# A graph network kernel: sheaves of 2048 sorted edges passed by one-hot products, in place of most row gathers

## The chip, the cores and the metric

The kernel runs on one core of a Trainium2 chip. The metric is device time in microseconds from start to end of one execution, median over runs; lower is better.

## The reference, cut to what matters

Four graph networks run one after the other on 6250 nodes of 128 features and 100,000 edges that are sorted by destination; each ends in a residual and a layer norm. Only the edge passing matters here:

```python
def _L0_gnn_ref(...):            # two passes of 64 features
    agg = jax.ops.segment_sum(h[src] * norm[:, None], dst, num_segments=n)
def _L1_gnn_ref(...):            # one pass of 128 features
    aggregated = jax.ops.segment_sum(x[src], dst, num_segments=num_nodes)
def _L2_gnn_ref(...):            # five layers of 128 features, with edge attributes
    for l in range(num_layer):
        m = jax.nn.relu(h[src] + edge_attr)
        agg = jax.ops.segment_sum(m, dst, num_segments=n)
def _L3_gnn_ref(...):            # two attention layers; the change leaves them alone
    ...
```

`src` is random, `dst` rises.

## The kernel before

Edges lie in 782 tiles of 128, nodes in 49 blocks of 128. A **pair** is an edge tile with a node block that it touches; there are at most 830, padded to 832, in 208 **groups** of four. A **stage** (one call of `_mixed`) is one edge passing: it reads a table of node rows in memory and adds into an aggregate in the SBUF. There are eight: two of 64 features ("narrow", L2225 and L2228), one of 128 (L2235) and five of 128 with attributes ("edge", L2261). Two attention stages (`_converse`, `_attend`) follow.

In a stage each group goes through the engines in this order. ACT copies four index columns (`index`, L1433). POOL issues four indirect DMAs, one per pair, each of which fetches 128 rows of the table (`fetch`, L1414). In edge stages SP loads four tiles of attributes (`load_attr`, L1387), DVE adds them (`join`, L1548) and ACT applies relu (L1450). ACT makes for each pair the matrix that tells which edge belongs to which node (`select`, L1441 to L1444). PE multiplies (`scatter`, L1509: four f32 matmuls, two instructions each) and DVE adds each pair's result to its node block (`add`, L1598). Rings of four buffers join the steps; semaphores named `index`, `gathered`, `joined`, `message`, `select`, `product` and `added` order them.

Some groups, 28 of 208 in a narrow stage and 18 in a wide one, fetch no rows by DMA. The table lies in the SBUF too, split into three bf16 terms (`first`, `second`, `high`, `middle`), and PE picks the rows with one-hot products: for each of the 49 blocks DVE makes a one-hot (L1580) and PE runs four matmuls of 384 (192) columns (`expand`, L1522); DVE sums the three terms (`merge`). These products are spread between the other groups' work. The groups of a stage's lead (10 or 12) run ahead of the loop while the table is split.

`_walk` finds the pairs and `_degree` counts degrees before the first stage; `_table` and `_norm` write a table to memory between stages. Each engine's work is a program of its own, in order, written out in the sequence in which it runs; `_hold` waits on a semaphore, with the target computed in a register inside loops. `_words` loads numbers from the SBUF into registers; such a number in an address (`bass.ds(where, 1)`) is computed in the sequencer.

## Time and profile before

| | us |
|---|---|
| median of 3 runs | 11302.24 (11300.65 to 11303.89) |
| the profiled execution, span | 11311.4 |
| PE busy | 8547.4 (76%) |
| DVE busy | 7592.0 (67%) |
| POOL busy | 7703.4 (68%) |
| ACT busy | 6350.9 (56%) |

The profiled execution is one run with the profiler on; its span is from the first to the last instruction and there is nothing of note around it, so it stands 9 us above the median. Busy time counts an engine's instructions. "PEld" is the loading of weights, which overlaps matmuls. "issue" after idle time means that the profile shows nothing that the engine waited for. Engine names with a q (PEldq, DVEq) are the sequencers, whose register work isn't counted as busy.

### The profile page before, as it was taken

The numbers are of one execution on the slowest core, as the hardware profiler recorded it, in microseconds if no ns is written. First come the engines' busy times: TensorE is split into PE (matmuls) and PEld (weight loads), VectorE is DVE, ScalarE is ACT, GpSimd is POOL, SyncE is SP. The second block draws the span as 40 slices with busy tenths as digits, with TensorE's granted clock in tenths as the row PEclk, the third lists the DMA queues.
The fourth block names the chain that finished last, engine by engine and source line by source line (L and its number), as shares of the span: only waits on it lengthen the run. The fifth ranks groups of instructions, "written<-read, shape, count | busy, mean of one in ns | idle before, by whom it ended". The sixth has DMA issues, their size and how long they took to land. (4 is left out here: it accounts for less than half of the span.)

```text
span 11311.4 us, 289275 instructions
## 1 busy us (share of the span) xinstructions
PE 8547.4 (76%) x56139; PEld 6348.4 (56%) x56140; DVE 7592.0 (67%) x21896; ACT 6350.9 (56%) x16860; POOL 7703.4 (68%) x7879
## 2 busy tenths in 40 slices
PE   5888688688868886887788688868886566656665
PEld 2777577555546554655555455645564455545554
DVE  5787678655557666776677666767775566746667
ACT  4444454444455555555555555555555666646774
POOL 2777777677757766775777577757773777657774
PEclk7999799799979997999899899989997787868887
DMA  2111111222234434443444344434443666546663
GB/s 57 31 31 30 38 32 31 53 56 56 55 92 111 110 92 113 112 111 89 116 110 111 96 110 111 112 95 112 111 108 101 180 193 193 149 132 189 197 194 113
DMA packets 1311535, 1169.02 MB, mean 103 GB/s; under 512 B 239258, under 2 KB 1106238, under 8 KB 1310224
## 3 DMA queue, kind: packets, MB, share of 16 engines
q0 software_dynamic: 272544, 566.00, 19.9%
q1 hardware_dynamic: 1038256, 596.28, 18.1%
q14 instruction: 647, 5.30, 0.1%
q8 instruction: 88, 1.44, 0.1%
HBM read 1009.04 MB, written 152.40 MB: 103 GB/s over the span
## 5 line engine op out<-in xcount | busy, mean ns | idle before, releaser
L1414 POOL DMA_INDIRECT rings<-rows_key,idx x4536 | 4361.0, 961 | 1919.5 <-issue 1333.9
L1598 DVE TENSOR_TENSOR bigDE<-bigDE,part 128x128 f32 (+1 forms) x6656 | 1891.0, 284 | 1398.1 <-PE part L1509 419.3
L1509 PE MATMUL part<-rings 128*128 128x128 f32 (+1 forms) x11920 | 1712.5, 290 | 658.8 <-ACT rings L1450 257.7
L1522 PE MATMUL wide<-bigDE,bigC 128*128 128x384 bf16 x10800 | 1951.6, 338 | 249.3 <-DVE bigC L1580 236.5
L696 POOL DMA_INDIRECT bigDE<-rows_key_value,idx x1664 | 1647.1, 990 | 691.1 <-issue 651.7
L1509 PEld LDWEIGHTS part<-rings 128*128 128x128 f32 (+1 forms) x11920 | 1556.8, 190 | 837.5 <-issue 759.1
L1441 ACT ACTIVATE rings<-iota,relK 128x128 f32<-128x128 f32 x5960 | 1900.4, 389 | 4.8 <-issue 1.5
L1414 POOL DMA_INDIRECT rings<-rows_hidden,idx x1424 | 1383.3, 971 | 595.4 <-issue 410.2
L1433 ACT COPY idx<-srcK 128x4 int32 (+1 forms) x1490 | 283.6, 191 | 2512.0 <-PE part L1509 2319.6
L1522 PEld LDWEIGHTS wide<-bigDE,bigC 128*128 128x128 bf16 x10800 | 1070.3, 101 | 989.3 <-issue 397.6
L1580 DVE TENSOR_SCALAR bigC<-bigC,node 128x512 bf16<-128x512 int16 x4410 | 1393.9, 380 | 43.9 <-issue 41.8
L1522 PE MATMUL wide<-bigF,bigC 128*128 128x384 bf16 x6840 | 1169.9, 326 | 168.0 <-DVE bigC L1580 165.3
L1444 ACT ACTIVATE rings<-rings,ones 128x512 f32<-128x512 f32 x1490 | 1075.6, 722 | 48.3
L1548 DVE TENSOR_TENSOR rings<-rings 128x512 f32<-128x512 f32 x945 | 655.1, 693 | 637.3 <-DMA rings<-rows_key,idx 612.7
L1522 PEld LDWEIGHTS wide<-bigF,bigC 128*128 128x128 bf16 x6840 | 653.3, 97 | 608.6 <-issue 195.9
L1522 PE MATMUL wide<-bigDE,rings 128*128 128x192 bf16 x9408 | 896.4, 254 | 106.1 <-DVE rings L1580 102.4
L812 PE MATMUL part<-bigB,rings 128*128 x3328 | 670.7, 363 | 357.0 <-ACT rings L723 226.1
L1522 PEld LDWEIGHTS wide<-bigDE,rings 128*128 128x128 bf16 x9408 | 799.7, 101 | 174.1 <-issue 159.8
L812 PEld LDWEIGHTS part<-bigB,rings 128*128 128x128 f32 x3328 | 576.8, 258 | 453.2 <-issue 452.6
L1580 DVE TENSOR_SCALAR rings<-W,node 128x512 bf16<-128x512 int16 x2352 | 742.7, 380 | 34.1 <-issue 34.1
L1450 ACT ACTIVATE rings<-rings 128x512 f32<-128x512 f32 x945 | 585.6, 620 | 310.5 <-DVE rings L1548 309.5
L713 ACT ACTIVATE rings<-iota,relK 128x128 f32<-128x128 f32 x1680 | 536.4, 390 | 0.0
(372 smaller groups left out, 10326.0 us busy)
## 6 DMA issues: line engine op xcount, KB each, us to landing
rings<-in_attr SPq DMA_DIRECT2D x3780, 64.0 KB
walk_value<-bigDE SPq DMA_DIRECT2D x416, 256.0 KB
rings<-walk_value SPq DMA_DIRECT2D x416, 256.0 KB
rings<-rows_key,idx POOLq DMA_INDIRECT x4536
bigDE<-rows_key_value,idx POOLq DMA_INDIRECT x1664
bigF<-in_attr SPq DMA_DIRECT2D x380, 64.0 KB
rings<-rows_hidden,idx POOLq DMA_INDIRECT x1424
rows_key<-rings SPq DMA_DIRECT2D x60, 320.0 KB, 2.6
```

What stands on the lines that cost most here:

```text
L696: e.indirect_dma_start(gbuf[:, g, r, :], None, table, bass.IndirectOffsetOnAxis(ap=c.idx[:, g, r:r + 1], axis=0)).then_inc(c.gathered[g].s ...
L713: e.activation(c.sel[:, g, r, :], c.iota[:, :], ACT.Abs, bias=c.relK[:, bass.ds(q * GROUP + r, 1)], scale=-1.0).then_inc(c.near.sem, 1)
L812: done = e.matmul(part[:, g % 2, r, 0:D + HEADS], turn[:, g % 2, r, :], query[:, bass.ds(where[r] * (D + HEADS), D + HEADS)], start=True, ...
L1414: e.indirect_dma_start(to[:, r, 0:width], None, table, bass.IndirectOffsetOnAxis(ap=idx[:, r:r + 1], axis=0)).then_inc(gate.sem, 16)
L1441: e.activation(to[:, r, :], c.iota[:, :], ACT.Abs, bias=c.relK[:, bass.ds(q * GROUP + r, 1)], scale=-1.0).then_inc(c.near.sem, 1)
L1444: e.activation(to, to, ACT.Relu, bias=c.ones[:, 0:1], scale=-1.0).then_inc(c.select.sem, 1)
L1450: e.activation(x, x, ACT.Relu).then_inc(c.message.sem, 1)
L1509: last = e.matmul(part[0:width, bank(n), r, :], msg[:, r, 0:width], sel[:, r, :], start=True, stop=True)
L1522: last = e.matmul(wide[:, r, 0:3 * width], hot[:, r * P:r * P + P], room.pieces(s, 1).rearrange("p a j f -> p (a j f)"), start=s == 0, sto ...
L1548: e.tensor_tensor(to, to, plus, ALU.add).then_inc(c.joined.sem, 1)
L1580: e.tensor_scalar(hots[(half * NODE_TILES + s) % depth], room.sources[half], c.node[:, s:s + 1], None, ALU.is_equal).then_inc(c.hot.sem, 1)
L1598: e.tensor_tensor(into, into, got, ALU.add).then_inc(c.added.sem, 1)
```

## The change

Of the 48 runs of 2048 edges (16 tiles) in the sorted list, the first 24 whose destinations span under 256 nodes become **sheaves**. The edges of a sheaf are sorted by their source block and laid out in 16 tiles of 128. Read in that order, a sheaf needs 16 + 48 = 64 steps, each a one-hot of 128 rows against one node block: 16 steps give each tile its first block, 48 the others, one each, in the tile in which that block begins. Three bf16 terms make 192 matmuls per sheaf. The results are drained to the SBUF, joined with attributes sorted the same way, and scattered to a window of 256 nodes by 16 f32 matmuls against marks made by DVE (`strike`), which `sum_up` adds to the aggregate. The other edges are 448 pairs in 112 groups (`LOOSE`), which go through the steps of before; 16 of these groups are the lead, four go beside each sheaf. The dense groups are gone.

New: `_lots`, once ahead of the first stage, finds the sheaves, sorts them (a rank per edge, then f32 one-hot products) and lists the steps. The first stage (`fresh=True`) makes the one-hots on DVE and also stores them, 256 KB per leg of 8 steps, 8 legs a sheaf; the other seven load them, into four buffers. `_arrange`, once ahead of the edge stages, gathers the sorted attributes by 384 indirect DMAs and stores them, 1 MB a sheaf. The pair lists of before are saved and loaded again for the attention stages, in `_project`. The load of the degree shares moves from the first to the third stage.

```diff
+LOT = 16
+SHEAVES = 24
+CANDIDATES = E // (LOT * P)
+SPAN = 256
+MARCH = LOT + NODE_TILES - 1
+LEGS = 8
+LEG = MARCH // LEGS
+HELD = 4
+LOOSE = -(-(EDGE_TILES - SHEAVES * LOT + NODE_TILES - 1) // GROUP)
+LBLOCKS = -(-LOOSE * GROUP // P)
+LCOLS = LBLOCKS * P
+HALF = 4
+BODY = 2 * HALF
+LEAD = LOOSE - SHEAVES * HALF
+QUEUE = SHEAVES * LOT
+QBLOCKS = QUEUE // P
...
+def _lots(c, ins, dram):
...
+            def belong(i):
+                e.wait_ge(c.spent.sem, c.spent.at(i - 1))
+                e.tensor_tensor(member[i % 2].rearrange("p (s a) -> p s a", a=LOT), deep(lots(block, i), n, LOT),
+                                wide(number[:, 0:n], n, LOT), ALU.is_equal).then_inc(c.hot.sem, 1)
+            belong(0)
+            for i in range(SHEAVES):
+                if i + 1 < SHEAVES:
+                    belong(i + 1)
+                sums, got, x = upto_s[i % 2], ps[:, i % 2, :, :], score[i % 2]
+                e.wait_ge(c.spent.sem, c.spent.at(i + 1))
+                e.wait_ge(c.chunked.sem, c.chunked.at(i - 1))
+                step(lambda: e.tensor_tensor_scan(sums[:, 0:half], ones, got[:, 2, 0:half], 0.0, ALU.mult, ALU.add))
+                e.tensor_tensor_scan(sums[:, half:cells], ones, got[:, 3, 0:half], sums[:, half - 1:half],
+                                     ALU.mult, ALU.add).then_inc(c.summed.sem, 1)
+                e.wait_ge(c.summed.sem, c.summed.at(i + 1))
+                step(lambda: e.tensor_tensor(x.rearrange("p (k x) -> p k x", k=2), got[:, 0:2, 0:half],
+                                             sums.rearrange("p (k x) -> p k x", k=2), ALU.add))
+                step(lambda: e.tensor_tensor(x, x, member[i % 2], ALU.mult))
+                e.tensor_reduce(lots(rank, i), x.rearrange("p (s a) -> p a s", a=LOT), AX.X, ALU.add
+                                ).then_inc(c.added.sem, 1)
+            e.wait_ge(c.added.sem, c.added.at(SHEAVES))
...
+            for i in range(SHEAVES):
+                e.wait_ge(c.hot.sem, c.hot.at(i + 1))
+                e.wait_ge(c.fed.sem, c.fed.at(i // 2 + 1))
+                e.wait_ge(c.chunked.sem, c.chunked.at(i - 3))
+                for a in range(LOT):
+                    last = e.matmul(ps[:, i % 4, 0:3 * LOT], hots[i % 2][:, a, :],
+                                    loads[i // 2 % 2][:, i % 2 * LOT + a, :, :].rearrange("p v x -> p (v x)"),
+                                    start=a == 0, stop=a == LOT - 1)
+                last.then_inc(c.spent.sem, 1)
...
+                if i % 2 == 0:
+                    m = i // 2
+                    e.wait_ge(c.fed.sem, c.fed.at(m))
+                    e.wait_ge(c.spent.sem, c.spent.at(2 * (m - 1)))
+                    here = slice(m * batch, (m + 1) * batch)
+                    _small(c, e, c.small_dve, 1, lambda: e.tensor_tensor(
+                        tile_hot, wide(high[:, here], batch, LOT), deep(number[:, 0:LOT], batch, LOT), ALU.is_equal))
+                    for v, x in enumerate(values):
+                        if v == 2:
+                            e.wait_ge(c.keyed.sem, c.keyed.at(2 * m + 2))
+                        e.tensor_tensor(loads[m % 2][:, :, v, :], tile_hot, wide(x[:, here], batch, LOT), ALU.mult
+                                        ).then_inc((c.fed if v == 2 else c.keyed).sem, 1)
+                e.wait_ge(c.spent.sem, c.spent.at(i - 1))
+                e.tensor_tensor(hots[i % 2], wide(lots(low, i), LOT, P), deep(c.iota[:, :], LOT, P), ALU.is_equal
+                                ).then_inc(c.hot.sem, 1)
...
+def _arrange(c, attr, out):
...
+            for i in range(SHEAVES):
+                got, kept = (g[i % depth] for g in gates)
+                if i >= depth:
+                    e.wait_ge(kept.sem, kept.at(16 * (i // depth)))
+                for a in range(LOT):
+                    e.indirect_dma_start(room[i % depth][:, a, :], None, attr,
+                                         bass.IndirectOffsetOnAxis(ap=c.edgeS[:, i * LOT + a:i * LOT + a + 1], axis=0)
+                                         ).then_inc(got.sem, 16)
...
+            def load_sheaf(i, h):
+                _hold(e, c.struck, lots(i, h, 0) - batches, c.tick_sp)
+                e.dma_start(room.msg[h], attr[1][bass.ds(i * 2 + h, 1), :, :, :].rearrange("a p t f -> (a p) t f")
+                            ).then_inc(c.sheaf[h].sem, 16)
+            def load_hots(i, h, k):
+                _hold(e, c.spent, legs(i, h, k) + (1 - HELD), c.tick_sp)
+                e.dma_start(room.hots[:, k % HELD, :],
+                            dram.hots[bass.ds(i * 2 + h, 1), k, :, :].rearrange("a p x -> (a p) x")
+                            ).then_inc(c.hotload[k % HELD].sem, 16)
...
+            def half(i, h):
+                for m in range(HALF):
+                    n = h * HALF + m
+                    if edge and real(i, n + RING):
+                        load_attr(i, n + RING)
+                    if edge and m == 0 and not initial(i, h):
+                        load_sheaf(i, h)
+                    if not initial(i, h, m):
+                        for leg in legs_of(i, h, m):
+                            supply(*leg)
...
+            def leg(i, h, k, hop):
+                if fresh:
+                    _hold(e, c.hot, (legs(i, h, k) + 1) * 2, c.tick_pe)
+                else:
+                    _hold(e, c.hotload[k % HELD], held(i, h, k) + 16, c.tick_pe)
+                for m in range(LEG):
+                    hot = room.hots[:, k % HELD, m * P:(m + 1) * P]
+                    x = k * LEG + m
+                    if x < LOT and x % batch == 0:
+                        _hold(e, c.drained, lots(i, h, x // batch) + (1 - batches), c.tick_pe)
+                    for j in (2, 1, 0):
+                        if x < LOT:
+                            terms = room.table[:, bass.ds(hop[m] * (3 * width) + j * width, width)]
+                            to = wide[:, x * P:x * P + width]
+                        else:
+                            at = ((x - LOT + 1) * 3 + j) * width
+                            terms = room.table[:, at:at + width]
+                            to = wide[:, bass.ds(hop[m] * P, width)]
+                        last = e.matmul(to, hot, terms, start=x < LOT and x % batch == 0 and j == 2,
+                                        stop=x >= MARCH - LOT, skip_group_check=True)
+                last.then_inc(c.spent.sem, 1)
+            def gather(i, h, m):
+                hop = nc.values_load_multi_w_load_instructions(
+                    hops[:, bass.ds(tiles(i * (MARCH // LOT), 0, 0) + (h * MARCH + m * LOT), LOT)], engines=[e.engine],
+                    min_val=0, max_val=NODE_TILES - 1 if m == 0 else LOT - 1,
+                    skip_runtime_bounds_check_because="block numbers and tiles of a sheaf")[1]
+                for k in range(2):
+                    leg(i, h, 2 * m + k, hop[k * LEG:(k + 1) * LEG])
+            def strike(i, h, b):
+                _hold(e, c.marked, tiles(i, h, (b + 1) * batch), c.tick_pe)
+                _hold(e, c.cleaned if edge else c.drained, lots(i, h, b) + 1, c.tick_pe)
+                if b == 0:
+                    _hold(e, c.lumped, i * 2 + (h - 1), c.tick_pe)
+                for a in range(b * batch, (b + 1) * batch):
+                    last = e.matmul(lump[0:width, h, 0:SPAN], room.msg[h][:, a, :], room.marks[:, a % 8, :],
+                                    start=a == 0, stop=a == LOT - 1)
+                last.then_inc(c.struck.sem, 1)
+            def half(i, h):
+                for m in range(HALF):
+                    scatter(i, h * HALF + m)
+                    gather(i, h, m)
+                    if m and exists(*earlier(i, h)):
+                        strike(*earlier(i, h), m - 1)
+                if exists(*earlier(i, h)):
+                    strike(*earlier(i, h), batches - 1)
...
+            def mark(i, h, b):
+                _hold(e, c.struck, lots(i, h, b) - 1, c.tick_dve)
+                for a in range(b * batch, (b + 1) * batch):
+                    e.tensor_scalar(room.marks[:, a % 8, :], c.wide_iota[:, :],
+                                    c.relS[:, bass.ds(tiles(i, h, a), 1)], None, ALU.is_equal).then_inc(c.marked.sem, 1)
+            def drain(i, h):
+                _hold(e, c.spent, legs(i, h, LEGS), c.tick_dve)
+                if edge:
+                    _hold(e, c.sheaf[h], i * 16 + 16, c.tick_dve)
+                else:
+                    _hold(e, c.struck, lots(i, h, 0) - batches, c.tick_dve)
+                for b in range(batches):
+                    to = room.msg[h][:, b * batch:(b + 1) * batch, :]
+                        e.tensor_tensor(to, banks[:, b, :, 0:width], to, ALU.add).then_inc(c.drained.sem, 1)
+                        e.tensor_copy(to, banks[:, b, :, 0:width]).then_inc(c.drained.sem, 1)
...
+            def sum_up(i, h, adds):
+                _hold(e, c.struck, lots(i, h, batches), c.tick_dve)
+                _hold(e, c.added, adds, c.tick_dve)
+                at = _words_one(nc, e, c.bases, i * 2 + h)
+                into = agg[0:width, bass.ds(at, SPAN)]
+                e.tensor_tensor(into, into, lump[0:width, h, 0:SPAN], ALU.add).then_inc(c.lumped.sem, 1)
+                _hold(e, c.lumped, i * 2 + (h + 1), c.tick_dve)
...
+            def half(i, h):
+                prior = earlier(i, h)
+                for m in range(HALF):
+                    n = h * HALF + m
+                    if edge and real(i, n + 2):
+                        join(i, n + 2)
+                    if fresh and not initial(i, h, m):
+                        for leg in legs_of(i, h, m):
+                            make_hots(*leg)
+                    if exists(*prior):
+                        mark(*prior, m)
+                    if m % 2 == 0:
+                        where = places(i, n)
+                    if m == 1 and exists(i - 1, h):
+                        sum_up(i - 1, h, q_of(i, n) * GROUP)
+                    adds(i, n, where[m % 2 * GROUP:m % 2 * GROUP + GROUP])
+                drain(i, h)
...
         _degree(c, F, dram)
+        _lots(c, ins, dram)
         h = slice(0, HID)
-        room = _narrow_room(c)
+        room = _room(c, C, HID)
         _table(c, B, hid, HID, other=F, op=ALU.mult, base=E_)
-        _mixed(c, "sum", hid, D_, HID, dram, room, begin=B,
-               weights=[(C, dram.share.rearrange("(a x) -> a x", a=1).to_broadcast([P, COLS]))])
+        _mixed(c, "sum", hid, D_, HID, dram, room, begin=B, fresh=True)
...
+        room = _room(c, C, D)
+        _arrange(c, ins["attr"].rearrange("t p f -> (t p) f"), sorted_attr)
...
```
## Rows read from the trace of the kernel before

**Rows 1.** The page's busy times, with share of the span and instructions.
```profile
span 11311.4 us, 289275 instructions
...
PE 8547.4 (76%) x56139; PEld 6348.4 (56%) x56140; DVE 7592.0 (67%) x21896; ACT 6350.9 (56%) x16860; POOL 7703.4 (68%) x7879
```

**Rows 2.** Groups by line on POOL: busy us, mean ns, idle before.
```profile
L1414 POOL DMA_INDIRECT rings<-rows_key,idx x4536 | 4361.0, 961 | 1919.5 <-issue 1333.9 <-ACT idx L1433 585.6
...
L1414 POOL DMA_INDIRECT rings<-rows_hidden,idx x1424 | 1383.3, 971 | 595.4 <-issue 410.2 <-ACT idx L1433 185.2
```

**Rows 3.** Timeline of POOL in an edge stage: start, us, idle before.
```profile
3612.08 0.94 POOL L1414 DMA_INDIRECT rings<-rows_key,idx  x1 [0.30 <-issue]
3613.33 0.94 POOL L1414 DMA_INDIRECT rings<-rows_key,idx  x1 [0.30 <-issue]
```

**Rows 4.** L1414 and L1598 by stage: duration ns, first and last start us.
```profile
L1414 POOL DMA_INDIRECT rings<-rows_hidden,idx x712: 940/944/3693, 222.5 to 1140.0; - x178
L1598 DVE TENSOR_TENSOR bigDE<-bigDE,part x832: 262/278/281, 237.0 to 1146.9; 64x128 f32 x167
...
L1414 POOL DMA_INDIRECT rings<-rows_key,idx x756: 940/944/1564, 2163.5 to 3116.6; - x189
L1598 DVE TENSOR_TENSOR bigDE<-bigDE,part x832: 268/287/290, 2173.2 to 3124.7; 128x128 f32 x167
...
L1414 POOL DMA_INDIRECT rings<-rows_key,idx x756: 938/944/3744, 3220.2 to 4194.4; - x189
L1598 DVE TENSOR_TENSOR bigDE<-bigDE,part x832: 267/286/290, 3240.8 to 4209.4; 128x128 f32 x167
```

**Rows 5.** Windows, edge and attention: PE, PEld, DVE, ACT, POOL busy; clock; DMA; GB/s.
```profile
3600.00:3800.00 200.00, 174.16 (x1125) 119.09 (x1123) 140.00 (x416) 115.46 (x295) 150.97 (x159) 0.97 0.41 111
...
9200.00:9400.00 200.00, 128.37 (x780) 111.32 (x780) 132.63 (x371) 147.98 (x444) 152.78 (x156) 0.87 0.70 204
```

**Rows 6.** Timeline of PE in a narrow stage, and at a loop's turn.
```profile
606.24 1.09 PE L1509 MATMUL part<-rings 128*64 128x128 f32 x8
607.26 2.81 PE L1522 MATMUL wide<-bigDE,rings 128*128 128x192 bf16 x32
610.00 1.09 PE L1509 MATMUL part<-rings 128*64 128x128 f32 x8
...
3601.52 1.44 PE L1522 MATMUL wide<-bigDE,bigC 128*128 128x384 bf16 x4 [0.58 <-issue]
```

**Rows 7.** Line L812, 9004.5 to 9005.7: matmuls and sequencer's address computations.
```profile
L812 PE MATMUL part<-bigB,rings x8: 276/277/376, 9004.7 to 9005.6; 128*128 x8
L812 PEldq FUSED_REGOPS  x4: 46/46/46, 9004.6 to 9005.0; - x4
```

**Rows 8.** Line L2172: instructions and address computations.
```profile
L2172 DVE TENSOR_TENSOR bigC<-bigC,settle x20: 812/814/821, 9908.9 to 11271.4; 128x640 f32 x16, 128x640 f32<-128x640 f32 x4
L2172 DVEq FUSED_REGOPS  x16: 57/57/57, 9908.4 to 11266.0; - x16
```

**Rows 9.** Line L563, register loads (8 words on DVE, 4 on PE).
```profile
L563 DVEq TENSOR_LOAD <-nRow x1046: 341/598/1330, 235.5 to 11226.6; - x175
...
L563 PEldq TENSOR_LOAD <-nRow x416: 327/414/1299, 8652.1 to 11067.5; - x139
```

**Rows 10.** Groups by form on DVE.
```profile
L1598 DVE TENSOR_TENSOR bigDE<-bigDE,part 128x128 f32 x4992 | 1429.1, 286 | 1046.2 <-PE part L1509 297.7 <-issue 178.5 <-DVE bigDE L1598 36.5
...
L2052 DVE TENSOR_SCALAR rings<-bigDE,rings 128x128 f32<-128x128 f32 x90 | 24.6, 342 | 8.0 <-PE turn L2105 4.6 <-DMA rows_key<-rings 3.3
L1566 DVE TENSOR_TENSOR bigDE<-bigDE,wide 128x256 f32<-128x256 f32 x56 | 23.6, 421 | 9.5 <-DVE bigDE L1564 1.8
...
L943 DVE TENSOR_TENSOR_SCAN bigDE<-bigF,small,bigDE 128x1024 f32<-128x1024 f32 x4 | 9.4, 2352 | 0.1
```

**Rows 11.** DMA issues: KB each, median us to landing.
```profile
bigC<-degree_share SPq DMA_DIRECT2D x1, 3200.0 KB, 12.0
```

**Rows 12.** Timeline of DVE in `_walk`.
```profile
34.13 0.52 DVE L342 TENSOR_TENSOR bigC<-bigB 128x343 f32<-128x343 f32 x1
```

942 lines of the change are left out of this document (650 added, 292 removed).

## The prediction

> **What bounds the kernel now.** I read the page first: PE is busy 76% of the span, DVE 67%, POOL 68%, ACT 56% [rows 1], so no engine bounds the whole by its share. The costliest group by line is the row gather, L1414, one indirect DMA per pair, in two forms with 4361.0 and 1383.3 us busy [rows 2]. The timeline of POOL inside a stage then shows these DMAs back to back: 0.94 us each and 0.30 us of "issue" between, 1.25 us from start to start [rows 3]. POOL's 68% is therefore a full engine: between two of its DMAs there is nothing that it waits for. The first and last start of L1414 and of the add L1598 give the length of each stage [rows 4]: 222.5 to 1147 us for a 64-wide one (925 us, of which 720 gathers x 1.25 = 900), 2163.5 to 3125 for the 128-wide sum (961; 760 x 1.25 = 950), 3220.2 to 4210 for an edge stage (990). Two, one and five such stages make 1850 + 961 + 4950 = 7761 us of 11311. Inside them PE is busy 174 us of 200 and DVE 140 [rows 5], close behind POOL: whatever frees POOL meets PE next.
>
> **What the change removes.** Every stage gathers 448 pairs instead of 720 or 760: POOL's part falls to 448 x 1.25 = 559 us. The dense path of 18 (28) groups goes too, with its 3528 (5488) matmuls and 882 (1372) one-hots made on DVE.
>
> **What it adds in a stage.** Sixteen groups run ahead of the sheaves at POOL's pace, 16 x 5.0 = 80 us. Then come 24 sheaves. For each, PE runs 64 steps of 3 bf16 matmuls of 128 (64) columns, 16 f32 matmuls of 256 columns (the strikes) and 4 scatters, while POOL does 16 gathers (20.0 us).
>
> Gather matmuls. No row has bf16 at 128 columns. The nearest is 192 columns: 32 matmuls from 607.26 to 610.00, 85.6 ns each, 80 of them columns at 2.4 GHz, so 5.6 above the columns [rows 6]. With the same addition 128 columns take 59 ns; bounds for the array are 59 and 85.6. But each of these matmuls has an address from a register. PE's sequencer shows its price at L812: four address computations of 46 ns start within 9004.6 to 9005.0 with four instructions between each two [rows 7], about 124 ns apart, so (124 - 46) / 4 = 20 ns per load or matmul instruction. One address plus one pair is 86 ns. The 16 first steps have three different addresses: 48 x 86 ns = 4.1 us. In the other 48 steps the three matmuls write to the same address. At L2172 input and output are two separate expressions of the same value, and 16 computations served 16 instructions [rows 8], so I take one computation for three: 46 + 6 x 20 = 166 ns per step, under the array's 3 x 61: 48 x 0.183 = 8.8 us. Sum 12.9 us; if nothing is shared, 192 x 86 ns = 16.5; if the array alone sets it, 11.3.
>
> The other work of a sheaf on PE: a scatter is 8 instructions of 128 columns in 0.9 to 1.0 us [rows 6], four are 3.6. A strike has twice the columns, 2 instructions of 213 ns: 16 x 0.44 = 7.1. Register loads: 4 words take 414 ns, 8 take 598 [rows 9], so 16 take about 1.0, four times a sheaf. They run in the sequencer; the strikes and scatters ahead of them keep the array busy for 2.6 us while the sequencer needs some 2.7 for its waits, its issue and the load. I leave 0.45 us open four times, 1.8 us. The loop's turn shows 0.58 us of "issue" on PE [rows 6]; with the waits inside the legs I take 1.0. Together 12.9 + 7.1 + 3.6 + 1.8 + 1.0 = 26.4, say 26.5 us: PE takes over from POOL's 20.0. Floor 11.3 + 7.1 + 3.6 = 22.
>
> DVE in the same time: 16 adds of 286 ns, some 0.4 from start to start, 6.4; 16 marks of 256 elements, between 0.27 (the 128-element row's busy time per instruction) and 0.42, taken at 0.4, 6.4; 4 joins and 4 drains of 0.69, 5.5; two register loads and gaps, 3 [rows 9, 10]. That is 21 us, under PE. The drain empties `wide`, which the next sheaf needs: 2.9 us, behind the eight strikes and the scatter that PE has in between (4.4 us); without them it would stand open, 24 x 2.9 = 70 us a stage. In the first stage DVE also makes the one-hots, 16 x 0.38 = 6 us more and no joins: 25 us, too near to PE's, and I add 1 us a sheaf.
>
> Transfers. A sheaf reads 2.1 MB of one-hots, in edge stages also 1.05 MB of sorted attributes, 1.05 of loose attributes and 1.05 of gathered rows, 5.2 MB. The attention stages move 204 GB/s [rows 5], so 26 us: level with PE, not above. But SP is one queue in order: `load_sheaf` waits until the strikes of the sheaf before last are done, and legs 2 and 3 of the one-hots stand behind it. 3200 KB took 12.0 us [rows 11], so 1 MB takes 4; the leg lands 2 + 4 + 1.3 and, with the gathers beside it, some 8.5 us after the wait ends, while PE needs it after 6. I take 2.5 us a sheaf in edge stages (bounds 0 and 5): 29 us.
>
> Stages, with 5 us at the start and 12 (edge: 17) for the last drain, clean and strikes: sum 5 + 80 + 24 x 26.5 + 12 = 733; first stage 757; edge 5 + 80 + 24 x 29 + 17 = 798. Saved: 925 - 757 + 925 - 733 + 961 - 733 = 588, and 5 x (990 - 798) = 960; together 1548 us.
>
> **What it adds outside.** `_arrange`: 384 gathers on POOL, 1.25 us each, 480, and 10 for the last transfer; nothing lies beside it: 490. `_lots`, by blocks: 10 us for three transfers; 95 small DVE steps, from 0.2 to 1.3 us by 1.07 ns an element over 0.15 (343 elements take 0.52, [rows 12]), 33; 14 gathers and a round trip of two rows through memory, 22; conversions and transposes 9; the ranks, per sheaf three elementwise steps and one reduction of 784 elements at 0.95 and 784 elements of scan at 2.3 ns [rows 10, 12], 5.8 and 0.5 for its waits, so 24 x 6.3 = 151; the ordering, per sheaf 2.3 for a one-hot of 2048 elements and 1.4 for its share of the loads, 4 x 24 = 96; the step lists 30; block boundaries 14. Sum 370 (300 to 460: scans and sync could be dearer). The reload of the pair lists in `_project` lies ahead of its first store and behind PE's work: nothing, at most 6.
>
> Total: 11311 - 1548 + 490 + 370 = 10623. The profiled run is 9 us over the median, so 10,614, say **10,620**.
>
> **A rule of the skill against it.** The 192-column row gives 5.6 ns above its columns [rows 6]. The Trainium skill, TensorE: Matmul & The Clock Gate, Back-to-back issue gap, says that a stream of load and matmul pairs sustains about 81 ns per matmul at N=128. By it the estimate for a sheaf's gathers would be 15.6 us, 2.7 us more than mine, and the estimate of the total some 500 us higher, about 11,120. No row here has that shape, so it stays open; it speaks for the rival of the dear pair below.
>
> **Rivals.** (1) PE keeps up: the array at 59 ns, no gaps, no late leg. Then 22 us a sheaf, stages of 5 + 80 + 528 + 12 = 625, saved 600 + 336 + 5 x 365 = 2761: 9,400. For it: the array's rates [rows 6]. Against: addresses cost the sequencer 46 ns each [rows 7], and SP's order stands in the code. Chance 0.12. (2) The dear pair: no address is shared, or the array needs 85.6 ns at 128 columns too. 3.6 us a sheaf more, x 192 = 690: about 11,300, hardly a change. For it: rows 7 show one computation per matmul; against: rows 8. Chance 0.18, a part of it with half the price. (3) Slower: PE's sequencer does not hide. Its four loads (4.0) and some 36 waits of 0.15 us (5.4) stand open in place of the 2.3 us that I left for them: 7.1 us a sheaf, 192 x 7.1 = 1363: about 11,980. It decides from 3.6 us a sheaf on, where 692 us of gain are spent. Against it: at L812 all four addresses are computed by 9005.0 while the matmuls start until 9005.6 [rows 7], so the sequencer runs ahead. Chance 0.14. (4) My forecast, 0.56, with a range of its own from 10,250 to 11,000.
>
> **The numbers.** Half of the case (1) lies between 9,400 and 9,900, a region left out; case (3) is left out above 11,400. The range is 9,900 to 11,400. Less than 0.2% (23 us) is about what a measurement of this kernel can tell from no change. Faster: 0.56 + 0.12 + 0.08 of (2) = 0.76; same 0.03; slower 0.14 + 0.07 of (2) = 0.21.
>
> **What the changed profile would show.** POOL's gathers at 448 a stage with idle time released by ACT, not "issue"; a 128-wide sum stage of 733 us and an edge stage of 798, so 65 us apart; PE busy over 90% of the sheaf stretches at a granted clock near 1; address computations on PE near 96 a sheaf (192 would be rival 2); PE waiting in edge stages for the transfer of the one-hots, in the leg two steps behind the start of a sheaf; 490 us of POOL alone ahead of the first edge stage; 370 us more, mostly DVE, ahead of the first stage. It would be wrong if matmuls of 128 columns stand over 94 ns apart, if the DMA share in edge stages comes to its ceiling well above 26 us a sheaf, or if the ranks take more than twice my 151.

## The result, and the profile after

The changed kernel takes 10390.29 us (10380.7 to 10403.5, 4 runs) beside 11303.06 for the kernel before: ratio 0.9193, 95% interval 0.918 to 0.9206. The forecast was 10,620, with a range of 9,900 to 11,400.

The page of the kernel after, with the lines that answer to [rows 1, 2]:

```profile
span 10388.3 us, 263193 instructions
PE 7573.6 (73%) x61770; PEld 6335.6 (61%) x61771; DVE 5550.2 (53%) x14642; ACT 4731.1 (46%) x12464; POOL 5758.3 (55%) x5865
...
L1913 POOL DMA_INDIRECT rings<-rows_key,idx x2688 | 2604.5, 969 | 2198.8 <-ACT idx L1926 1420.8
L2027 PE MATMUL wide<-bigDEF,bigC 128*128 128x128 bf16 (+2 forms) x32256 | 2422.0, 224 | 129.4 <-issue 77.3
```

POOL's gathers (L1913) had "issue" ahead of them in [rows 2]; now most of their idle time ends with ACT's index copy, which itself waits for TensorE. The bound has passed to PE. Windows of an edge stage and of the 128-wide sum (PE, PEld, DVE, ACT, POOL busy; granted clock; DMA share; GB/s), beside [rows 5]:

```profile
3600.00:4200.00 600.00, 574.95 (x5655) 515.13 (x5653) 327.39 (x914) 291.99 (x714) 344.99 (x362) 0.93 0.63 194
2260.00:2860.00 600.00, 577.86 (x5712) 518.32 (x5712) 269.37 (x817) 196.31 (x540) 344.55 (x366) 0.92 0.40 119
```

PE is busy 96% of the time, POOL 57%. The length of a sheaf is read from the register loads of the block lists, four a sheaf. L2032 in the two narrow stages, the 128-wide sum and the first edge stage (duration ns, first and last start):

```profile
L2032 PEldq TENSOR_LOAD <-pairs x96: 1102/1107/1546, 733.4 to 1350.4; - x96
...
L2032 PEldq TENSOR_LOAD <-pairs x96: 1102/1107/1132, 1484.8 to 2081.3; - x96
...
L2032 PEldq TENSOR_LOAD <-pairs x96: 1102/1107/1127, 2252.0 to 2884.6; - x96
...
L2032 PEldq TENSOR_LOAD <-pairs x96: 1102/1106/1122, 3582.0 to 4218.3; - x96
```

A stage's 96 loads have 95 intervals, four to a sheaf: (4218.3 - 3582.0) / 95 x 4 = 26.8 us in the edge stage (26.8 to 27.1 in the five), 26.6 in the sum, 26.0 and 25.1 in the first and the second narrow one. The forecast had, in the same order, 29, 26.5, 27.5 and 26.5. The first and second narrow stage, the sum and the edge stages last 724, 704, 739 and, in the mean of five, 754 us, from the first gather (L1913) to the last sum of a sheaf (L2112), where I had 757, 733, 733 and 798. The first edge stage as an example:

```profile
L1913 POOL DMA_INDIRECT rings<-rows_key,idx x448: 938/944/3707, 3483.9 to 4199.8; - x150
```
```profile
L2112 DVE TENSOR_TENSOR bigDEF<-bigDEF,lump x24: 405/408/422, 3639.9 to 4235.2; 128x256 f32 x24
```

Against [rows 4] that saves 201 + 221 + 222 + 5 x 236 = 1824 us, 276 more than forecast. `_arrange` (L1028) has 384 gathers from 2996.1 to 3474.2 us, 488 us with its last transfer, against 490. `_lots` takes 419 (first row gather at 641.6, at 222.5 in [rows 4]), against 370. 1824 - 488 - 419 = 917; the profiled executions differ by 923.

```profile
L1028 POOL DMA_INDIRECT bigC<-in_attr,W x384: 940/944/988, 2996.1 to 3474.2; - x192
```

Where a sheaf's 26.8 us go is in the timeline of PE in the edge stage:

```profile
3700.87 1.05 PE L2005 MATMUL part<-rings 128*128 128x128 f32 x8
3701.76 2.84 PE L2027 MATMUL wide<-bigDEF,bigC 128*128 128x128 bf16 x48
3704.44 1.95 PE L2045 MATMUL lump<-bigDEF,bigC 128*128 128x256 f32 x8
3706.22 1.05 PE L2005 MATMUL part<-rings 128*128 128x128 f32 x8
3707.11 2.84 PE L2027 MATMUL wide<-bigDEF,bigC 128*128 128x128 bf16 x48
...
3713.30 1.05 PE L2005 MATMUL part<-rings 128*128 128x128 f32 x8
3714.19 2.40 PE L2027 MATMUL wide<-bigDEF,bigC 128*128 x24
3716.96 1.66 PE L2027 MATMUL wide<-bigDEF,bigC 128*128 x12 [0.36 <-issue]
3718.77 1.72 PE L2027 MATMUL wide<-bigDEF,bigC 128*128 x12 [0.15 <-issue]
3720.98 2.04 PE L2005 MATMUL part<-rings 128*128 128x128 f32 x8 [0.49 <-issue]
3722.81 3.61 PE L2027 MATMUL wide<-bigDEF,bigC 128*128 128x128 bf16 x48
3726.26 1.95 PE L2045 MATMUL lump<-bigDEF,bigC 128*128 128x256 f32 x8
```

Three things are to be seen, all from start to start. A gather of the later steps takes 2.68 us for 48 matmuls, 56 ns each. The first gather of a sheaf, with an address of its own for each matmul, takes 6.79 us (3714.19 to 3720.98), 141 ns each. And behind it the next scatter takes 1.83 us instead of 0.89 and the next gather 3.45 instead of 2.68. That is work at the lower of the clock's two levels, 1.2 GHz, for part of the time: the scatter takes twice as long, and the mean granted clock of the stage is 0.93. A strike of 4 matmuls, 8 instructions, takes 1.78 us, as forecast.

### The profile page after: what moved, and what is told of

Same layout as the page of the kernel before. It is cut to its first block and busy times, and to the rows that moved or that the text cites. A ratio compares the mean times of both kernels' runs of the same rounds, so it can differ in the third digit from the quotient of the medians.

```text
span 10388.3 us, 263193 instructions
## 1 busy us (share of the span) xinstructions
PE 7573.6 (73%) x61770; PEld 6335.6 (61%) x61771; DVE 5550.2 (53%) x14642; ACT 4731.1 (46%) x12464; POOL 5758.3 (55%) x5865
## 5 line engine op out<-in xcount | busy, mean ns | idle before, releaser
L1913 POOL DMA_INDIRECT rings<-rows_key,idx x2688 | 2604.5, 969 | 2198.8 <-ACT idx L1926 1420.8
L2027 PE MATMUL wide<-bigDEF,bigC 128*128 128x128 bf16 (+2 forms) x32256 | 2422.0, 224 | 129.4 <-issue 77.3
L2027 PEld LDWEIGHTS wide<-bigDEF,bigC 128*128 128x128 bf16 x32256 | 2090.8, 103 | 467.2 <-issue 240.7
L1187 POOL DMA_INDIRECT bigDEF<-rows_key_value,idx x1664 | 1645.4, 989 | 687.1 <-issue 654.0
L2130 DVE TENSOR_TENSOR bigDEF<-bigDEF,part 128x128 f32 (+1 forms) x3584 | 1018.0, 284 | 1382.3 <-PE part L2005 873.2
L1913 POOL DMA_INDIRECT rings<-rows_hidden,idx x896 | 860.0, 960 | 553.4 <-ACT idx L1926 299.1
L1933 ACT ACTIVATE rings<-iota,pairs 128x128 f32<-128x128 f32 x3584 | 1144.0, 389 | 3.2
L2091 DVE TENSOR_SCALAR bigDEF<-iota,rows 128x256 f32<-128x256 f32 x2304 | 697.3, 366 | 659.5 <-PE lump L2045 658.6
L2045 PE MATMUL lump<-bigDEF,bigC 128*128 128x256 f32 x3840 | 905.9, 384 | 0.6
L2045 PEld LDWEIGHTS lump<-bigDEF,bigC 128*128 128x128 f32 x3840 | 702.5, 190 | 83.6 <-DVE bigDEF L2091 2.6
L1204 ACT ACTIVATE rings<-iota,pairs 128x128 f32<-128x128 f32 x1680 | 536.5, 390 | 0.0
L1028 POOL DMA_INDIRECT bigC<-in_attr,W x384 | 362.3, 944 | 177.5 <-issue 116.7
L1946 ACT ACTIVATE bigC<-bigC 128x512 f32<-128x512 f32 x480 | 283.1, 622 | 268.1 <-DVE bigC L2103 268.1
```

What stands on the lines that cost most here:

```text
L1187: e.indirect_dma_start(gbuf[:, g, r, :], None, table, bass.IndirectOffsetOnAxis(ap=c.idx[:, g, r:r + 1], axis=0)).then_inc(c.gathered[g].s ...
L1204: e.activation(c.sel[:, g, r, :], c.iota[:, :], ACT.Abs, bias=c.relK[:, bass.ds(q * GROUP + r, 1)], scale=-1.0).then_inc(c.near.sem, 1)
L1913: e.indirect_dma_start(gbuf[:, n % RING, r, 0:width], None, table, bass.IndirectOffsetOnAxis(ap=c.idx[:, n % RING, r:r + 1], axis=0)).then ...
L1933: e.activation(to[:, r, :], c.iota[:, :], ACT.Abs, bias=c.relL[:, bass.ds(q * GROUP + r, 1)], scale=-1.0).then_inc(c.near.sem, 1)
L2027: last = e.matmul(to, hot, terms, start=x < LOT and x % batch == 0 and j == 2, stop=x >= MARCH - LOT, skip_group_check=True)
L2045: last = e.matmul(lump[0:width, h, 0:SPAN], room.msg[h][:, a, :], room.marks[:, a % 8, :], start=a == 0, stop=a == LOT - 1)
```

## The experiments

Four theories. **A**: the first gather of a sheaf is set by PE's sequencer, which works out one address per matmul. **C**, the stronger form that e3 led to: the sequencer's whole work of a sheaf is nearly as long as the sheaf, so that work added to it or taken from it shows in the time. The rivals: **B**, the first gather waits for other engines; **D**, outside the first gather PE's array (its matmuls and weight loads) sets the pace.

**e1: no addresses in the first gather.** The kernel takes the table block of each of the first 16 steps as a constant, so its sums are those of other blocks.

```diff
-                            terms = room.table[:, bass.ds(hop[m] * (3 * width) + j * width, width)]
+                            terms = room.table[:, x * (3 * width) + j * width:x * (3 * width) + (j + 1) * width]
```

> Left out: in the first 16 steps of a sheaf the table block of tile x is always block x, so no address comes from a register there; the sums are those of other blocks. Theory A (the sequencer sets the first 16 steps: an address, a load and a matmul every 124 to 138 ns, 6.8 us for 48 matmuls where the other steps take 2.7, and the TensorE clock falls behind it and stays low for some 1.7 us more of work): a sheaf loses 4.1 + 1.7 = 5.8 us and meets POOL's 20.0, so 26.9 becomes 21 to 22 us; total about 10390 - 192 x 5.3 = 9,370 us, granted clock of the edge stages 0.98. Theory B (those steps are slow because they wait for the emptied accumulators and for one-hots): no change, 10,390.

Measured: 9756.07 us (one run; before 11306.39 on the same chip). The first gather's list was no longer loaded either, so three loads make a sheaf. Line L2032 in the sum stage and in the first edge stage, and a window of the latter:

```profile
L2032 PEldq TENSOR_LOAD <-pairs x72: 1102/1106/1119, 2114.1 to 2621.9; - x72
...
L2032 PEldq TENSOR_LOAD <-pairs x72: 1101/1106/1134, 3323.3 to 3882.6; - x72
```
```profile
3350.00:3850.00 500.00, 462.53 (x5434) 437.73 (x5433) 313.14 (x877) 274.79 (x679) 329.97 (x344) 1.00 0.71 222
```

A sheaf takes (2621.9 - 2114.1) / 71 x 3 = 21.5 us in the sum stage, 5.2 less, and 23.6 in the edge stage, 3.2 less; the granted clock is 1.00. Theory A holds in kind, and in the sum stage in size; B falls, since the waits for other engines stand in the gather as before. The total misses A's 9,370 by 386 us. The first stage falls only from 26.0 to 24.6 us a sheaf, where PE now waits for DVE's marks (L2091, 51.1 us in the stage) and for row gathers (27.0 us), and the edge stage meets something else, which the timeline of PE there names:

```profile
3704.81 2.85 PE L2027 MATMUL wide<-bigDEF,bigC 128*128 128x128 bf16 x48 [1.71 <-DMA bigC<-sheaf_hots]
```

The second gather waits for its one-hots. That fits the late leg of the forecast, 23.6 - 21.5 = 2.1 us a sheaf where I had 2.5; in the changed kernel the slow first gather covers it. Whether it is late for its place behind `load_sheaf` or for the 222 GB/s that the stage moves, no run separates: none has both e1's edit and another order on SP.

**e2: the attribute load moved behind the legs.**

```diff
-                    if edge and m == 0 and not initial(i, h):
+                    if edge and m == 2 and not initial(i, h):
```

> The load of the sorted attributes on SP stands two positions later in the sheaf, behind the one-hots of legs 2 to 5. Theory of the forecast (legs 2 and 3 come 2.5 us late behind it): 24 x 5 x 2.5 = 300 us less, 10,090. Theory now, from the sheaf period of 26.9 us in edge stages against 26.6 in the stage without attributes: the late leg hardly exists, 24 x 5 x 0.0 to 0.3 = 0 to 36 us less, 10,355 to 10,390.

Measured: 10411.62 us (10384.19 to 10419.71), ratio to before 0.9206 (0.9193 to 0.9219); the changed kernel has 0.9193 (0.918 to 0.9206). The intervals overlap, so there is no difference, as the second theory had it: in the changed kernel nothing waits for that leg.

**e3: two strikes woven into the first gather.** A strike is issued one tile at a time ahead of every second step. The kernel has e2's edit too, as have e8, e10 and e12.

```diff
+                    if between is not None and m % 2 == 0:
+                        between(m // 2)
...
+                    of = ((i - 1, h, batches - 1), (*earlier(i, h), 0))[k]
+                    woven = m == 0 and exists(*of[0:2])
+                    leg(i, h, 2 * m + k, hop[k * LEG:(k + 1) * LEG], (lambda t: tile(*of, t)) if woven else None)
...
-                    if m and exists(*earlier(i, h)):
+                    if m >= 2 and exists(*earlier(i, h)):
                         strike(*earlier(i, h), m - 1)
-                if exists(*earlier(i, h)):
-                    strike(*earlier(i, h), batches - 1)
```

> Two of the four strikes of a sheaf (four f32 matmuls of 256 columns each, no address) are issued between the steps of its first gather, and the attribute load stands two positions later. Theory A (sequencer): while the sequencer computes addresses the array has strikes to do, 2.7 + 3.6 = 6.3 us of array beside 6.7 us of sequencer, in place of 6.8 + 3.6; 3.5 us a sheaf less, and 1.7 more where the clock no longer falls: 26.9 becomes 21.7 to 23.4 us; total 9,400 to 9,720, I take 9,550. Theory B (the first gather waits for other engines): the strikes only move; 10,390, or more by the strikes' own waits for DVE's marks and ACT's clean, up to 1 us x 192 = 10,580.

Measured: 10205.19 us (10200.78 to 10217.71), ratio 0.903 (0.9016 to 0.9043), faster than the change by 1.8%: 185 us where A had 840. A sheaf of an edge stage takes 25.8 us, not 21.7 to 23.4. The timeline of PE shows where the rest went:

```profile
3721.16 0.60 PE L2050 MATMUL lump<-bigDEF,bigC 128*128 128x256 f32 x2
...
3725.40 0.67 PE L2050 MATMUL lump<-bigDEF,bigC 128*128 128x256 f32 x2 [0.69 <-ACT bigC L1946]
...
3729.83 1.13 PE L2005 MATMUL part<-rings 128*128 128x128 f32 x8 [0.48 <-issue]
3731.40 2.85 PE L2029 MATMUL wide<-bigDEF,bigC 128*128 128x128 bf16 x48 [0.44 <-issue]
...
3735.90 2.85 PE L2029 MATMUL wide<-bigDEF,bigC 128*128 128x128 bf16 x48 [0.54 <-issue]
```

The clock stays up. But the woven gather with its two strikes takes 8.67 us (3721.16 to 3729.83) where A had 6.3 to 6.7, 0.69 of them a wait for ACT's relu (L1946), and the next scatter and the two gathers behind it now have about half a microsecond of "issue" ahead of them. The strikes that had stood there had covered the sequencer's waits and list loads: that is how I read it, and it led to theory C.

**e4: the sorting gathers spread over the sum stages.** `_arrange` goes; POOL issues its gathers between those of the rows, in groups of four, through free parts of a ring, and SP stores each group.

```diff
+            def gather_more(i, k):
+                _hold(e, c.keyed, group_of(i, k) - base_w + 1, c.tick_pool)
+                if not isinstance(i, int) or i:
+                    _hold(e, c.kept[k], i * 16, c.tick_pool)
+                for r in range(GROUP):
+                    e.indirect_dma_start(slots[k][:, r, :], None, source,
...
-        _arrange(c, ins["attr"].rearrange("t p f -> (t p) f"), sorted_attr)
```

> The 384 gathers that sort the attributes stand no longer by themselves ahead of the edge stages; 96, 144 and 144 of them are issued on POOL inside the three sum stages, 4, 6 and 6 a sheaf. Theory A (POOL is no longer the bound in a stage, its 16 gathers x 1.25 = 20.0 us lie beside 25 to 27 us of TensorE): 490 us go; 20 x 1.25 = 25.0 against 26.0 costs nothing, 22 x 1.25 = 27.5 against 25.1 and 26.6 costs 24 x (2.4 + 0.9) = 79; total about 9,980. Rival (POOL's gathers still set the stage, through loose pairs that come late): every gather costs its 1.25 us wherever it stands, 10,390.

Measured: 10015.05 us (10002.72 to 10021.48), ratio 0.8861 (0.8848 to 0.8875). The list loads (here L2077) of the second narrow stage, the 128-wide sum and the first edge stage:

```profile
L2077 PEldq TENSOR_LOAD <-pairs x96: 1102/1107/1838, 1502.5 to 2162.2; - x96
...
L2077 PEldq TENSOR_LOAD <-pairs x96: 1102/1107/1941, 2339.1 to 2996.9; - x96
...
L2077 PEldq TENSOR_LOAD <-pairs x96: 1102/1106/1126, 3201.6 to 3844.0; - x96
```

These are 27.8 and 27.7 us a sheaf: with 22 gathers a sheaf POOL is the bound again at 22 x 1.25 = 27.5. The edge stage stays at 27.0. With 20 gathers the first stage takes 26.8 for 26.0, where no cost was expected. POOL was indeed idle for a part of every sheaf: the move takes away 490 us of POOL alone and costs some 110 us in the sum stages, and the total, 9,980 expected, is 375 us shorter.

**e5 to e10: runs in which the streams stall.** Beside these six the kernel before took 14,555 us (e5 to e8) and 14,574 us (e9 and e10), on two chips. Unchanged edge stages took 33.3 to 34.1 us a sheaf, with stretches such as this one (timeline of PE, e9), while 47 matmuls in a row lasted as long as elsewhere:

```profile
4319.14 0.22 PE L2030 MATMUL wide<-bigDEF,bigC 128*128 128x128 bf16 x1
4320.55 2.78 PE L2030 MATMUL wide<-bigDEF,bigC 128*128 128x128 bf16 x47 [1.19 <-issue]
```

So they are compared among themselves only, by sheaf, and a difference under 0.8 us, which unchanged stages show among themselves, says nothing. Why they stall was not tried. Nor is it shown that it belongs to the chip: e12, beside which the kernel before took 11,303.82 us, ran under the same chip number as e9 and e10.

```diff
+                for _ in range(4):
+                    _hold(e, c.select, q_of(i, h * HALF + m) + 1, c.tick_pe)
```

> Ahead of each of a sheaf's four gathers TensorE waits four more times for a semaphore that has long been reached, 16 waits a sheaf; a wait with its tick took the sequencer 0.244 us from start to start. Theory C (not the array but the sequencer's whole work of a sheaf is the bound: 96 addresses x 0.131 = 12.6 us, four register loads 4.4, waits, loads and matmuls the rest): 16 x 0.244 = 3.9 us a sheaf show nearly whole, 192 x 3 to 3.9 = 580 to 750 us more, 10,970 to 11,140. Theory D (only the first gather is bound by the sequencer, elsewhere it runs ahead of the array and hides them): only 4 of 16 show, 192 x 1 = 190 us more, 10,580.

```diff
-                            to = wide[:, bass.ds(hop[m] * P, width)]
+                            to = wide[:, bass.ds(hop[m] * P + (j * 16 if width < P else 0), width)]
```

> In the two narrow stages the three matmuls of a later step write to three different addresses (16 columns apart; their sums are wrong), so each has an address of its own: 192 computations a sheaf for 96. Rival 2 of the forecast priced at 20 ns an instruction would give 96 x 46 ns = 4.4 us a sheaf, 211 us in all; with the 0.131 us from one address to the next that the trace of the changed kernel shows, 48 later steps go from about 0.125 to 0.39 us, 12.7 us a sheaf more, 24 x 2 x 12.7 = 610 us: 11,000. If the address is hidden by the array: 10,390.

```diff
-                    if x < LOT and x % batch == 0:
-                        _hold(e, c.drained, lots(i, h, x // batch) + (1 - batches), c.tick_pe)
+                    if x == 0:
+                        _hold(e, c.drained, lots(i, h, 0), c.tick_pe)
```

> The first gather waits once for all four batches of accumulators to be emptied, in place of once per batch: three waits a sheaf fewer in the stretch that the sequencer sets. Theories A and C (sequencer): 3 x 0.244 = 0.73 us less a sheaf, if the fourth batch is empty by then (2.9 us of drain under 4.4 us of strikes and scatter), 192 x 0.73 = 140 us less, 10,250. Rival (the wait for the fourth batch costs more than the three waits): same or up to 100 us slower.

> The woven strikes and the spread sorting gathers together. The spread alone gave 10,015; weaving gave 1.1 us a sheaf in edge stages, 24 x 5 x 1.1 = 130 us; in the sum stages POOL is the bound with 22 gathers a sheaf (27.7 us), so nothing there: 9,885. If the two gains simply add up: 10,015 - 183 = 9,830.

Measured: 12867.89, 12886.65, 12471.75 (12443.16 to 12498.23) and 12324.54 us (12285.95 to 12356.87). By sheaf in the first edge stage: 36.4 with 16 waits more, 34.1 in e6, whose edge stages are unchanged, 34.5 with one wait for four, 33.2 with the woven strikes. The unshared narrow stage takes 40.4, the same stage of e7, which has e7's own edit, 29.8: 10.6 more, of the expected 12.7 us for two addresses a step more. The waits show at 2.3 of 3.9 us. The one wait for four saves nothing here, where 0.73 us were expected; whether it costs something, 34.5 beside 34.1 can't tell. Whether the gains of e3 and e4 add can't be read from e8.

**e9 and e11: another edit in each stage, with the stalls and without.** Both have the edits of e5, e6 and e7, and these: the block lists loaded twice, 12 of the 16 strike matmuls of a sheaf left out, and half of the matmuls of the ordering in `_lots` left out.

```diff
+                if mode == "loads":
+                    again = load()
+                    hop = [(hop, again)[t % 2][t] for t in range(LOT)]
...
-                for a in range(b * batch, (b + 1) * batch):
+                for a in range(b * batch + (batch - 1 if mode == "strikes" else 0), (b + 1) * batch):
...
-                for a in range(LOT):
+                for a in range(0, LOT, 2):
                     last = e.matmul(ps[:, i % 4, 0:3 * LOT], hots[i % 2][:, a, :],
```

> One kernel with another edit in each stage, read by the time from one sheaf to the next; the first stage and the first edge stage are unchanged and are the control (26.0 and 26.9 us in the changed kernel). Stage 2 (narrow): three addresses a later step, the two low terms' sums land elsewhere. Sum stage of 128 and fourth edge stage: 12 of the 16 strike matmuls of a sheaf are left out. Second edge stage: 16 more waits a sheaf. Third edge stage: one wait for the emptied accumulators in place of four. Fifth edge stage: each block list is loaded twice. In the ordering of the sheaves ahead of stage 1, 8 of 16 matmuls a sheaf are left out. Theory C (the sequencer's work is what bounds a sheaf): stage 2 from 25.1 to 36 us; strikes out: the array loses 5.4 us and the sequencer under 1, so 26.6 and 26.9 become 25 to 26; 16 waits: 26.9 + 2.8 to 3.9 = 30; one wait: 26.9 - 0.7 = 26.2, or + 1 for the fourth batch; loads twice: + 3 to 4.4 = 30 to 31. Theory D (the array bounds all but the first gather): strikes out 21.5, 16 waits 27.9, loads twice 26.9 to 28, stage 2 as under C. Ordering: if TensorE bounds it, 155 us become about 100, DVE's pace.

> The kernel with another edit in each stage once more. In its first run the streams of all engines stood still for 0.6 to 1.2 us about every hundred instructions, in unchanged stages too (34.1 us a sheaf in the unchanged edge stage where the changed kernel had 26.9), and an edit that adds or removes instructions moved those stalls along. On a chip without them, with 26.9 as control: theory C (sequencer) strikes out 25 to 26, 16 waits 29.5 to 30.8, lists loaded twice 30 to 31.3; theory D (array outside the first gather) strikes out 21.5, 16 waits 27.9, lists twice 27 to 28; one wait for four 26.2 under both.

e9 took 12646.76 us; e11 10734.28, with 11300.8 before. The list loads of e11 (L2036): unshared narrow stage, sum without strikes, then the five edge stages in order (control, 16 waits, one wait, strikes out, lists loaded twice, so eight loads a sheaf):

```profile
L2036 PEldq TENSOR_LOAD <-pairs x96: 1101/1107/1148, 1407.3 to 2359.1; - x96
...
L2036 PEldq TENSOR_LOAD <-pairs x96: 1101/1106/1133, 2535.2 to 3142.6; - x96
...
L2036 PEldq TENSOR_LOAD <-pairs x96: 1102/1107/1127, 3833.0 to 4473.2; - x96
...
L2036 PEldq TENSOR_LOAD <-pairs x96: 1101/1107/1128, 4670.4 to 5349.4; - x96
...
L2036 PEldq TENSOR_LOAD <-pairs x96: 1102/1106/1128, 5545.6 to 6158.6; - x96
...
L2036 PEldq TENSOR_LOAD <-pairs x96: 1101/1106/1124, 6351.4 to 6979.3; - x96
...
L2036 PEldq TENSOR_LOAD <-pairs x192: 1100/1104/1122, 7174.1 to 7906.6; - x192
```

| us a sheaf | e11 | against (narrow and sum: the changed kernel; edge: e11's control) | e9 |
|---|---|---|---|
| control, edge | 27.0 | | 34.1 |
| three addresses a step, narrow | 40.1 | 25.1 | 40.6 |
| strikes out, sum | 25.6 | 26.6 | 30.7 |
| strikes out, edge | 26.4 | 27.0 | 31.3 |
| 16 waits more, edge | 28.6 | 27.0 | 36.6 |
| one wait for four, edge | 25.8 | 27.0 | 34.5 |
| lists loaded twice, edge | 30.7 | 27.0 | 38.8 |

12 strike matmuls a sheaf are 5.3 us of array, and leaving them out gives 0.5 to 1.1: D falls. Loading the lists twice adds 4.4 us to the sequencer alone, and 3.7 show, which speaks for C. The 16 waits show at 1.6 of 3.9, between C's 2.6 to 3.9 and D's 1.0, so not all of the sequencer's work shows. One wait for four gives 1.2 where 0.73 were expected; the clock, below, has a part in it. 96 more addresses cost 15.0 us, 156 ns each, where rival 2 of the forecast had 3.6 us a sheaf for them. The timeline of PE in e11's edge stage without strikes shows what takes the place of the array's work:

```profile
6607.88 1.13 PE L2005 MATMUL part<-rings 128*128 128x128 f32 x8
6609.52 2.85 PE L2030 MATMUL wide<-bigDEF,bigC 128*128 128x128 bf16 x48 [0.51 <-issue]
...
6613.83 1.13 PE L2005 MATMUL part<-rings 128*128 128x128 f32 x8 [0.54 <-issue]
6615.78 1.69 PE L2030 MATMUL wide<-bigDEF,bigC 128*128 x12 [0.82 <-DVE bigC L2114]
...
6623.71 2.04 PE L2005 MATMUL part<-rings 128*128 128x128 f32 x8 [0.48 <-issue]
```

The scatter takes 1.64 us from start to start instead of 0.89, the one before the first gather 1.95, and the first gather 7.93 instead of 6.79. The 0.82 us ahead of the first gather are no work of the sequencer's: PE waits for DVE's drain (L2114), which has fewer strikes before it to hide behind. PE's waits for it make 21.7 us in this stage and 4.4 in the control, 0.7 us a sheaf. Part of what is given back is the clock: 0.83 in this stage beside 0.92 in the control, and 0.99 in the stage with one wait for four (windows of e11):

```profile
3900.00:4400.00 500.00, 482.17 (x4717) 432.05 (x4716) 268.11 (x755) 240.52 (x589) 278.71 (x293) 0.92 0.64 192
...
5600.00:6100.00 500.00, 480.39 (x4964) 429.00 (x4963) 283.63 (x791) 254.41 (x620) 296.47 (x310) 0.99 0.67 204
6450.00:6950.00 500.00, 442.31 (x4331) 374.23 (x4328) 273.88 (x766) 242.23 (x598) 287.09 (x299) 0.83 0.65 196
```

So three things stand in for the 5.3 us of strikes: the sequencer, the drain and the clock. How much is sequencer and how much clock these runs don't separate. For the ordering in `_lots`, the matmuls (L883) of the kernel after and of e11, which leaves half of them out:

```profile
L883 PE MATMUL ordered<-bigC,bigDEF x768: 413/413/449, 437.3 to 601.0; 128*128 128x48 f32 x192
```
```profile
L883 PE MATMUL ordered<-bigC,bigDEF x384: 413/413/449, 436.3 to 521.5; 128*128 128x48 f32 x192
```

164 us become 85, DVE's pace of 3.5 us a sheaf (it is busy 80 of the 85): in the changed kernel TensorE sets this stretch, at 213 ns an instruction and a granted clock of 0.50.

> The woven strikes and the spread sorting gathers together, on another chip than the one on which the kernel before took 14,555 us, whose sheaf periods can't be set beside the others. As before: 10,015 - 130 = 9,885; 9,830 if the gains add.

Measured: 12338.71 us (12296.15 to 12373.92), again beside 14,574, so whether the two gains add stayed unmeasured here too.

**e12: the best of them together.** The edits of e2, e3 and e4, and the waits for emptied accumulators in pairs:

```diff
-                    if x < LOT and x % batch == 0:
-                        _hold(e, c.drained, lots(i, h, x // batch) + (1 - batches), c.tick_pe)
+                    if x < LOT and x % (2 * batch) == 0:
+                        _hold(e, c.drained, lots(i, h, x // batch) + (2 - batches), c.tick_pe)
```

> The woven strikes, the spread sorting gathers, and in the first gather two waits for the emptied accumulators in place of four. Edge stages: 25.7 us a sheaf woven, the sequencer's own work by the stages without strikes (25.6); two waits of 0.244 us fewer give 25.2, so 24 x 5 x (26.9 - 25.2) = 204 us less than the spread kernel's 10,015; sum stages stay at POOL's 22 gathers, 27.7. Total 9,810. If the fused waits hold up the sequencer for the second batch instead (up to 1 us a sheaf): 9,930. On a chip on which the streams stall (kernel before 14,555 us): about 12,250.

Measured: 9829.03 us (9820.06 to 9835.55), ratio to before 0.8696 (0.8681 to 0.871), the change having 0.9193. Its list loads (L2079) in the 128-wide sum and the first edge stage:

```profile
L2079 PEldq TENSOR_LOAD <-pairs x96: 1102/1107/1871, 2345.7 to 3003.2; - x96
...
L2079 PEldq TENSOR_LOAD <-pairs x96: 1102/1107/1134, 3210.5 to 3811.9; - x96
```

25.3 us a sheaf in the edge stage against the expected 25.2, and 27.7 in the sum stage, POOL's pace, as expected; the total was to be 9,810.

## Why the prediction was right, step by step

- **What the change removes.** Right: POOL's gathers no longer set a stage, PE does, 96% busy. e4 shows it from the other side: six more gathers a sheaf cost 1 to 3 us, not 7.5. What sets PE's own pace is for a large part its sequencer, as the next points show.
- **A sheaf on PE, 26.5 us.** The sum was right (26.6 in the sum stage) by luck: errors of opposite sign cancel. Terms, forecast and measured in the timeline of the edge stage: later gathers 8.8 and 8.0 without the clock (I had put 61 ns a matmul there where my own row gave 59, which is 0.3 of the 0.8); first gather 4.1 and 6.8; strikes 7.1 and 7.1; scatters 3.6 and 3.6; gaps and loop turn 2.8 and none outside the first gather in that sheaf; and 1.7 us at the lower clock, which I had not reckoned with. That is 4.4 us too little in two terms and 3.6 too much in two others. The term that was mis-sized most is the first gather, by the price of an address, 86 ns for address, load and matmul from [rows 7]. There four instructions stand between two addresses that are 124 ns apart, and I gave each of them a share. In the first gather only two stand between, and the matmuls are still 141 ns apart: the time hangs on the address, hardly on the number of instructions. e1, without these addresses, shows it.
- **Sharing of one address by three matmuls** [rows 8]. Right, and decisive: the trace has 18432 address computations at L2027 (first line at the end of this section), which is 96 for each of 192 sheaves and not 192, and without the sharing a sheaf of a narrow stage takes 15.0 us more (e11). At that price 24 x 8 x 15.0 = 2880 us in all eight stages would have been far more than the whole gain.
- **The sequencer hides.** Right in the number, wrong in the mechanism. I left it 2.3 us open and nearly none shows as idle time, since strikes or scatters stand ahead of every load. But with 5.3 us of array work taken out a sheaf still takes 25.6 to 26.4 (e11), and with 4.4 us of loads added 3.7 more. The mechanism of rival 3 was nearer than its chance of 0.14 says, though its 7.1 us a sheaf did not come.
- **The late leg, 2.5 us a sheaf in edge stages.** It did not appear (26.8 against 26.6): 5 x (798 - 754) = 220 of the 276 us by which the stages beat the forecast. In e1 a wait of 2.1 us a sheaf for the one-hots is there, once the first gather is quick. My need at 6 us (two scatters of 0.9 and 4.1) rested on the same address price; with 0.9 + 6.8 + 1.8 it comes at 9.5, behind the 8.5 of the arrival.
- **First stage, 1 us a sheaf for DVE's one-hots.** 26.0 against 25.1, right in size; both narrow stages are some 1.5 us a sheaf shorter than forecast, for which no run here looks for the cause.
- **`_arrange`.** Right, 488 for 490.
- **`_lots`.** The ranks were right in the sum: the 24 reductions (second line there) start 6.3 us apart, though one takes 1.46 us where I had 0.95. The ordering took 164 us for my 96, since I had DVE's work and not the matmuls', 32 instructions of 213 ns at the lower clock level. This term was 68 us too small; all the others together came out some 20 shorter. (My list adds up to 365; the 370 is rounded up.)
- **The skill's rule.** The Trainium skill, TensorE: Matmul & The Clock Gate, Back-to-back issue gap, has about 81 ns a matmul at N=128 for load and matmul pairs. Measured here: 56 ns at the higher clock level, 48 in 2.68 us. The 5.6 ns above the columns of [rows 6] is 2.5 here, so the page's rule did not bear on the time, and rival 2's dear pair falls.

```profile
L2027 PEldq FUSED_REGOPS  x18432: 46/46/66, 734.8 to 7561.6; - x199
...
L860 DVE TENSOR_REDUCE rings<-bigDEF x24: 1459/1459/1460, 283.5 to 428.5; 128x16 f32<-128x784 f32 x24
```

## What to carry to other kernels

Add up an engine's sequencer as a second engine: addresses, waits and register loads each in its own row, and ask which array work stands beside them; a share of 96% busy says nothing of which of the two sets the pace. Price an address from a register by the spacing of addresses in a stretch where nothing else is the bound, and let operands share one where they can. When a change frees an engine, move work of it that stands alone into the freed time: the best single step beyond the change was to put 490 us of POOL's sorting gathers into stages in which POOL had become partly idle. And when a sum comes out right, compare its terms: here errors of opposite sign hid each other.

## What the hardware showed that I had not expected

- After a gather of 48 matmuls at 141 ns each the scatter and a part of the gather behind it ran at the lower clock level, 1.7 us longer together, although PE counts as busy; with the address-free gather the granted clock is 1.00 (e1), and with every strike but four matmuls out it falls to 0.83 (e11).
- A register load of 16 words took 1.107 us on PE.
- A wait with its tick, ALU instruction to ALU instruction, took 0.244 us where the sequencer did nothing else, and showed at 0.10 each in a sheaf (16 for 1.6 us, e11).
- Beside e5 to e10 the same kernel before ran 29% slower, and their traces have stretches of 0.6 to 1.2 us of "issue" in unchanged code, with runs of matmuls as long as elsewhere. An edit that won without these stalls (one wait for four, 27.0 to 25.8) won nothing with them (34.1 and 34.5); the cause stays open.
